# One branch for the whole feed-forward stage instead of one in every product, the weights' remainders no longer stored, and another written-out order of work

## What is computed

```
for layer 0:  x = x + ga * attention(LN(x)*(1+ca)+sa)       # 16 heads, causal, LN on q and k
              x = x + gb * ffn0(LN(x)*(1+cb)+sb)            # ternary weights, hidden size 1024
              # ffn0: h = silu(w1 h)*(w2 h); h = gelu(h1 h); h = gelu(h2 h); w3 h
for layer 1:  x = x + ga * scan_block(LN(x)*(1+ca)+sa)      # selective scan, 512 channels, 16 states
              x = x + gb * ffn1(LN(x)*(1+cb)+sb)            # block-quantised activations and weights
```

## Time and profile before

| | us |
|---|---|
| median of 3 runs | 4162.34 (4157.99 to 4164.06) |
| the profiled execution, its own time | 4167.61 |
| its span, first to last instruction | 4165.8 |
| mean granted TensorE clock in it | 0.932 of full speed |

### The profile page before, as it was taken

How to read it: one execution, slowest core, us unless ns; L and a number is a source line. 1 busy time by engine, 2 the same in 40 slices (tenths; PEclk the granted TensorE clock), 3 DMA queues, 4 the chain that set the end, 5 groups by cost and what they waited for, 6 DMA issues and landing times. The chain is left out here.

```text
span 4165.8 us, 50421 instructions
## 1 busy us (share of the span) xinstructions
PE 3523.9 (85%) x16621; PEld 2034.0 (49%) x16621; DVE 3318.2 (80%) x3646; ACT 2583.4 (62%) x3703; POOL 2716.0 (65%) x1960
## 2 busy tenths in 40 slices
PE   5687888989899998989898898989999898989513
PEld 3263645546373645546373554636364554636201
DVE  4514878989798888979797887979898897979694
ACT  2345566767667676766666676767667676666431
POOL 0132866768595876768595776759586776768563
PEclk9799999999999999999999999999999999999756
DMA  4630201102030301103030211203030211203000
GB/s 164 258 105 15 97 21 62 62 26 97 6 117 1 97 26 61 62 21 102 6 102 17 82 41 46 77 8 115 1 107 16 76 46 41 82 6 102 0 5 5
DMA packets 69435, 247.81 MB, mean 59 GB/s; under 512 B 9472, under 2 KB 10112, under 8 KB 68736
## 3 DMA queue, kind: packets, MB, share of 16 engines
q1 hardware_dynamic: 66816, 235.35, 16.8%
q10 hardware_dynamic: 2304, 8.39, 0.5%
HBM read 212.25 MB, written 31.46 MB: 59 GB/s over the span
## 5 line engine op out<-in xcount | busy, mean ns | idle before, releaser
L671 POOL TENSOR_TENSOR kept<-kept,hb 128x512 f32<-128x512 f32 x640 | 811.0, 1300 | 71.1 <-DVE hb L1925 70.9
L1916 DVE TENSOR_TENSOR_SCAN hb<-ps,hb 128x512 f32<-128x512 f32 x640 | 745.0, 1205 | 17.5 <-ACT ps L1362 12.7
L929 PE MATMUL ps<-hid_bhi,wring 128*128 128x512 f32 x1536 | 628.0, 409 | 70.9 <-issue 53.6
L929 PE MATMUL ps<-hid_blo,wring 128*128 128x512 f32 x1536 | 619.8, 404 | 0.0
L1362 ACT ACTIVATE ps<-kept,a_neg 128x512 f32<-128x512 f32 x640 | 423.0, 690 | 174.4 <-DVE hb L1916 174.4
L929 PE MATMUL ps<-hid_ahi,wring 128*128 128x512 f32 x1280 | 516.7, 404 | 8.0 <-POOL hid_alo L686 8.0
L639 POOL TENSOR_TENSOR kept<-kept,hb 128x1024 f32<-128x1024 f32 x128 | 300.2, 2360 | 336.3 <-DVE hb L1860 297.7
L929 PE MATMUL ps<-hid_alo,wring 128*128 128x512 f32 x1280 | 505.0, 395 | 0.0
L632 POOL TENSOR_SCALAR_AFFINE_SELECT room<-room 128x512 f32<-128x512 f32 x256 | 217.7, 862 | 427.2 <-ACT room L1569 427.2
L1988 DVE TENSOR_REDUCE room<-ps 128x4 f32<-128x2048 f32 (+3 forms) x256 | 375.2, 1486 | 123.6 <-PE ps L1105 111.3
L1925 DVE TENSOR_TENSOR hb<-hb,ps 128x512 f32<-128x512 f32 x640 | 404.0, 673 | 0.1
(11 more groups left out here) (198 smaller groups left out, 7359.2 us busy)
## 6 DMA issues: line engine op xcount, KB each, us to landing
wring<-w_hi SPq DMA_DIRECT2D x352, 512.0 KB, 3.3
kept<-in_wffn SPq DMA_DIRECT2D x22, 512.0 KB, 6.3
w_hi<-wring SPq DMA_DIRECT2D x22, 512.0 KB, 7.0
w_lo<-wrest SPq DMA_DIRECT2D x22, 512.0 KB, 5.2
xn<-in_x_fm SPq DMA_DIRECT2D x17, 512.0 KB, 3.3
out_fm<-xc ACTq DMA_DIRECT2D x16, 512.0 KB, 5.4
room<-in_wmod SPq DMA_DIRECT2D x2, 1536.0 KB, 8.1
win<-in_win SPq DMA_DIRECT2D x1, 1024.0 KB, 8.4
```

The costliest lines, as they stand in the source:

```text
L671: pool.tensor_tensor(acc[:, m, :], acc[:, m, :], hb[:, s % 8, :], ALU.add).then_inc(acc_done, 1)
L929: mm = pe.matmul(bank(bk), wring[:, r % 3, at + k * P:at + (k + 1) * P], src[i][:, k, :], start=(k == 0 and i == 0), stop=(k == K - 1 and ...
L1916: dve.tensor_tensor_scan(hb[:, s % 8, :], bank(2 + m % 2), hb[:, s % 8, :], 0.0, ALU.mult, ALU.add).then_inc(scanned, 1)
```

## The change

- `w_lo` and its stores go. DVE subtracts in place in `stage`; a slot of `stage` is loaded again when it has been measured, not when it has been split; ACT's rounding of tile t also waits until tile t-3 has been split; the store of tile t-1 stands behind the load of tile t (before: the stores of tile t-2).
- The branch moves out of `product`. The whole stretch of PE's list from `up(0)` to `mid(17)` with the scan's `spread` and the next pass's `next_mean` and `next_var` is a function, written twice: for `has_rest > 0` with the raw float32 weights in place of the fp32r ones, and behind it, as the other arm, for `has_rest` of 0 as before. One branch in a pass chooses. SP's list has one branch in a pass likewise.
- The loads of the first three tiles stand at the end of SP's list for the first pass and no longer in `find_flag`. SP no longer waits for `acc_init` and `u_ready` ahead of the tiles.
- All four written-out lists get another order.

Its core, cut:

```
-        wrest = sb("wrest", [P, 2, HM * P], F32R)
+        wraw = sb("wraw", [P, 2, HM * P])
-        w_lo = nc.dram_tensor("w_lo", (FT, P, HM * P), F32).ap()
...
         def split_sync(sp):
-            for t in range(FT + 2):
+            for t in range(FT + 1):
                 if t < FT:
                     if t >= 3:
-                        sp.wait_ge(w_split, t - 2)
+                        sp.wait_ge(w_measured, t - 2)
                     sp.dma_start(stage[:, t % 3, :], a["wffn"][t]).then_inc(stage_loaded[t % 3], 16)
-                if t >= 2:
-                    r = t - 2
+                if t >= 1:
+                    r = t - 1
                     sp.wait_ge(w_rounded, r + 1)
                     sp.dma_start(w_hi[r], wring[:, r % 3, :].bitcast(F32)).then_inc(hi_stored[r % 3], 16)
-                    sp.wait_ge(w_split, r + 1)
-                    sp.dma_start(w_lo[r], wrest[:, r % 2, :].bitcast(F32)).then_inc(lo_stored[r % 2], 16)
...
         def split_act(act, t):
...
+                    act.wait_ge(w_split, t - 2)
...
-                dve.tensor_tensor(wrest[:, t % 2, :], stage[:, t % 3, :], wring[:, t % 3, :].bitcast(F32), ALU.subtract).then_inc(w_split, 1)
+                dve.tensor_tensor(stage[:, t % 3, :], stage[:, t % 3, :], wring[:, t % 3, :].bitcast(F32), ALU.subtract).then_inc(w_split, 1)
...
+            def wait_tile(r, exact):
+                if exact:
+                    pe.wait_ge(w_loaded[r % 3], since(w_loaded[r % 3], 16 * (r // 3 + 1)))
+                else:
+                    pe.wait_ge(raw_loaded[r % 2], since(raw_loaded[r % 2], 16 * (r // 2 + 1)))
+
-            def product(bk, r, at, src, K, fresh=None):
+            def product(bk, r, at, src, K, exact, fresh=None):
                 for k in range(K):
-                    if k == K - 1:
-                        with pe.If(has_rest > 0):
...
                     for i in range(2):
+                        cols, x = slice(at + k * P, at + (k + 1) * P), src[i][:, k, :]
+                        if exact:
+                            w = wring[:, r % 3, cols]
+                        else:
+                            w, x = wraw[:, r % 2, cols], x.bitcast(F32)
+                        mm = pe.matmul(bank(bk), w, x, start=(k == 0 and i == 0), stop=(k == K - 1 and i == 1))
...
+            if ffn:
+                with pe.If(has_rest > 0):
+                    feed_forward(False)
+                with pe.Else():
+                    feed_forward(True)
```

More of the change, by code:

```diff
@@ L511, in build @@
         for i in range(2):
-            each("ffn", 16 * len(range(i, FT, 2)), rest_loaded[i])
+            each("ffn", 16 * len(range(i, FT, 2)), raw_loaded[i])
         each("pre", 1, xd_done, xd_split, dt_exp, dt_log, dt_ready)
@@ L1194, in tensor_pass @@
             scores_turned(0, 1)
+            in_proj(0)
             tail_spread(1, 2)
-            in_proj(0)
+            scores(1, 2)
             in_proj(1)
-            scores(1, 2)
+            scores_turned(0, 2)
+            turn_max(1)
             in_proj(2)
-            scores_turned(0, 2)
+            tail_spread(0, 3)
+            scores(2, 0)
             values(0, 0)
-            values(0, 1)
-            turn_max(1)
-            tail_spread(0, 3)
-            values(0, 2)
-            scores(2, 0)
-            row_sums(0)
             in_proj(3)
@@ L1213, in tensor_pass @@
             dt_proj(0)
+            values(0, 1)
+            values(0, 2)
+            row_sums(0)
             dt_proj(1)
+            scores_turned(1, 1)
             dt_proj(2)
-            scores_turned(1, 1)
             dt_proj(3)
             scores(2, 2)
+            head_spread(0, 0)
             values(1, 0)
-            head_spread(0, 0)
             scores_turned(1, 2)
@@ L1230, in tensor_pass @@
             scores(3, 1)
+            fin_var()
+            values(1, 1)
+            scores_turned(2, 1)
             values(1, 2)
-            fin_var()
-            scores_turned(2, 1)
+            scores(3, 2)
             row_sums(1)
-            scores(3, 2)
             fin_turn(0)
-            head_spread(0, 1)
             scores_turned(2, 2)
+            values(2, 0)
+            fin_turn(1)
             turn_max(3)
-            values(2, 0)
             scores_turned(3, 0)
@@ L1243, in tensor_pass @@
             values(2, 2)
+            row_sums(2)
             scores_turned(3, 1)
-            row_sums(2)
-            fin_turn(1)
+            values(3, 0)
             scores_turned(3, 2)
-            head_spread(1, 1)
-            att_proj(0)
-            values(3, 0)
+            head_spread(0, 1)
             values(3, 1)
@@ L1297, in tensor_pass, with feed_forward @@
-            mid(11)
-            mid(12)
-            spread(0, 10)
-            spread(1, 9)
-            mid(13)
-            mid(14)
-            spread(1, 10)
-            mid(15)
-            spread(0, 11)
-            next_mean()
-            mid(16)
-            next_var()
-            spread(1, 11)
-            mid(17)
+            def feed_forward(exact):
+                up(0, exact)
+                up(1, exact)
+                up(2, exact)
+                spread(0, 3)
+                up(3, exact)
+                up(4, exact)
+                spread(0, 4)
+                spread(1, 3)
+                up(5, exact)
+                up(6, exact)
+                up(7, exact)
+                mid(0, exact)
+                mid(1, exact)
+                spread(0, 5)
+                spread(1, 4)
+                mid(2, exact)
+                mid(3, exact)
+                spread(1, 5)
+                spread(0, 6)
+                mid(4, exact)
+                mid(5, exact)
+                mid(6, exact)
+                spread(0, 7)
+                spread(1, 6)
+                mid(7, exact)
+                spread(1, 7)
+                mid(8, exact)
+                spread(0, 8)
+                mid(9, exact)
+                mid(10, exact)
+                spread(1, 8)
+                spread(0, 9)
+                mid(11, exact)
+                mid(12, exact)
+                spread(1, 9)
+                mid(13, exact)
+                spread(0, 10)
+                mid(14, exact)
+                mid(15, exact)
+                next_mean()
+                spread(0, 11)
+                mid(16, exact)
+                next_var()
+                spread(1, 10)
+                mid(17, exact)
+                spread(1, 11)
@@ L2049, in vector_pass @@
             tail_in(0, 0)
-            pick_mod()
             find_max(0, 0)
             tail_scan(0, 0)
+            find_max(0, 1)
+            split(0)
             normalise(2)
-            split(0)
-            find_max(0, 1)
             split(1)
@@ L2150, in vector_pass @@
             gate_up(5)
+            gate_up(6)
             times_c(3, 0)
-            gate_up(6)
+            gate_up(7)
             times_b(4, 0)
-            gate_up(7)
             times_b(4, 1)
             scan(3, 1)
+            times_c(3, 1)
+            pick_next()
             scan(4, 0)
-            times_c(3, 1)
-            scan(4, 1)
             times_c(4, 0)
```

348 lines of the change are left out of this document (150 added, 198 removed).

## The result

The changed kernel takes 4308.8 us (median of 4 runs, 4308.0 to 4314.0), the kernel before 4163.2 beside it: a ratio of 1.035, 95% interval 1.032 to 1.037. It is 145.6 us slower, and 187 above the forecast of 4122.

A forecast was written before the change was run, and what follows sets the result against it. No engine full throughout: PE, DVE and POOL together limit the feed-forward half, chains between engines the attention half. 4167.6 - 12.5 - 0 - 21 - 7 = 4127.1, 4122 against the median; range 4080 to 4166.

The forecast's parts named there:

- Splitting, -12.5: Weight splitting in the first pass: without w_lo's stores ACT waits less for loads, -12.5 us, ends -18 and +9.
- Removed branches, 0: PE's 34 branches a pass in the products: off the path, removal gives 0, at best -1.2 us a pass.
- The jump, covered, 0: PE's far branch ahead of up(0): 3.47 us, covered by the wait for POOL's split, cost 0, end +3.47 a pass.
- rival 1: Jump ahead of up(0) not covered, PE late and at half clock: 70 us more, 4192; chance 0.11.
- Start of the feed-forward half, -21: Shorter PE wait ahead of up(0) keeps full clock: 1.5 us a pass, 21 us in 14 passes.
- Head and tail together -0.5 us a pass: Attention half, new order at its two ends: 7 us gained in 14 passes, ends -3.6 and +2.4 a pass.
- Head: Start of the attention half: shift_q(0) directly ahead of tail_in(1,0), DVE loses an estimated 0.5 us.
- Tail: find_max(3,2) to weigh(3), 26.1 us: about 1 us less, with 2.4 us of new waiting for copy_head(1).
- Rival 2: Attention half: a wait at row_sums(2) or head_in costs more than counted, +2.4 a pass, 4163; chance 0.12.

The follow-up runs named there:

- old_lists: The changed kernel with the four lists of the kernel before: 4167.1 us, ratio 1.000.
- store_later: start_only with SP's store of w_hi in the splitting issued two tiles behind the load, not one: 4139.4 us, ratio 0.994.
- first_old: The changed kernel with the old four lists in the first pass alone: 4279.0 us, ratio 1.027.
- lists_only: The kernel before, its code kept, with the four lists of the changed kernel: 4308.6 us, ratio 1.035.
- start_only: old_lists with only the new start of the feed-forward half (fin_cols, fin_ff(0) and ff_add(0) later): 4141.5 us, ratio 0.995.
- silu_and_first: The changed kernel with gate_silu(3) ahead of exp_probs(0,1) again and the old lists in the first pass: 4205.1 us, ratio 1.010.
- silu_first: The changed kernel with one ACT item moved, gate_silu(3) ahead of exp_probs(0,1) again: 4240.2 us, ratio 1.018.
- silu_late: The kernel before with one ACT item moved, gate_silu(3) behind exp_probs(0,1): 4228.4 us, ratio 1.016.

## Why the prediction was wrong, step by step

- **Splitting, -12.5.** Mis-sized: old_lists starts its first up(0) 3.6 us earlier (217.7 against 221.3), and even these don't show in its time. The step took ACT's waiting to shrink with the traffic; store_later shows that it follows the slots, which DVE and the lists set free. And the sum left out that the new lists move the splitting's hooks: in the changed kernel up(0) came 26.4 us later, and first_old gives 29.7 back.
- **Removed branches, 0.** Right: lists_only has all 34 a pass and the time of the changed kernel, old_lists has none and the time of the kernel before.
- **The jump, covered, 0.** Right: 3.36 us a pass, finished 1.0 us ahead of the split's end (0.5 us ahead of up(0) was forecast), and 80 us when exposed (70 for rival 1, clock included). The rule that the forecast cites from the Trainium skill, Runtime: NRT & Kernel Launch, section Instruction fetch mechanics, that a taken branch to a target outside the pages held has to fetch it, agrees with these rows.
- **Start of the feed-forward half, -21.** Right, in the mechanism too: in the changed kernel PE waits 1.0 us ahead of up(0) in all 14 full passes, the clock is 1.00, and the halves are together 17.9 us shorter. That start_only's 25.6 come near the 21 is in part luck: in the profiled executions its attention halves gained nearly as much on old_lists as its feed-forward halves did.
- **"Head and tail together -0.5 us a pass".** This is the step that failed.
  - Head: +2.6, not +0.5. The walk counted what stands between shift_q(0) and find_max(1,0), and not that shift_q(0) itself had moved behind normalise(3) and pre_centre, with a wait of 0.79 us for PE. The expectations blame ACT's square(2), now behind the four items of tail_decay(0). DVE's normalise(2), which needs it, starts without idle time (2544.86, behind find_max(0,1)); whether it delays project_v(1) is not shown.
  - Between head and tail the sum had no term: the items there were taken as unmoved in effect. One swap in it, gate_silu(3) behind exp_probs(0,1), costs 68.6 us, and the rest of the new middle 2.9 us up to find_max(2,2), or 4.2 with the old head.
  - Tail: the wait for copy_head(1) came as priced (2.47 us for 2.4), but 3.3 of the 26.1 us to beat came with the half clock and are no wait of the order.
  - Nor has the clock a term outside the start. In the middle the changed kernel's attention halves differ by up to 3.7 us with it; in the tail, where the changed kernel keeps full clock, it gives some 3 us back.
- **Rival 2** named the right half and side, at two places that did no harm that shows, and bounded it at +2.4 us a pass; the attention half grew by 5.7 to 9.4.

The account, in medians: swap and first pass 103.7 (silu_and_first); the rest of the new order against start_only 4205.1 - 4141.5 = 63.6; the new start with the new code 4141.5 - 4163.2 = -21.7. These are steps of one chain of kernels, so they sum to the 145.6 by construction; another order of steps would share it out otherwise.

Of the swap, the Trainium skill bears on it: ScalarE: Activation LUTs, section Table sets: the hidden batching unit, says that functions of different sets cost a load at each change between them. The trace agrees, two loads of 1.28 us for one exponential among silus. But 2.6 us of loads are not the 4.9 us a pass (68.6 / 14): the fourth silu waits for the loads and for the exponential of 1.88 us, PE waits for the silu, and the clock falls behind that wait. In passes with little difference in clock the swap costs 3.2 to 3.5 us (silu_first, silu_late); the rest comes and goes with the half clock.

Open: why the clock falls in some passes and not in others with the same lists, in the tail, ahead of up(0) and in the middle; and which part of the new feed-forward order loses the 7 us at the end.

start_only and store_later beat both kernels: 4141.5 and 4139.4 us, 0.5 and 0.6% under the kernel before.

## What to carry to other kernels

When a whole issue order is rewritten, walk every stretch of it with the inputs of each item from the other engines' lists; a stretch without a term in the sum is not a stretch that costs nothing. Before a list is blamed or praised for a wait, look at the granted clock in that window and compare passes at the same clock. Search an order for single items first: three moved items gave all of the gain here, and one moved item almost half of the loss.

## What the runs showed of the hardware

- A change of ACT's table shows as one load of 1.28 us, with the next instruction 0.02 us behind it (2986.43, 1.28, then 2987.73). The page ScalarE: Activation LUTs of the Trainium skill, section What ACT_TABLE_LOAD costs, adds a drain of about 1.38 us to each; these rows show none, so 1.3 us a change is what counts here.
- A far taken branch on PE costs 3.3 to 3.9 us in every pass (16 in each run), also when the same arm was entered one pass earlier.
- The same 7 us of the tail ran at clock 0.50 or 1.00, 28 matmuls or 60, in passes with the same lists, with 26.1 and 22.8 us for the stretch around them: single passes of one kernel differ by more than the new start is worth (1.4 us a pass).
